# Gating the rows before the experts, one bank for the sum of all experts, and value sums in transpose mode

## The reference, cut to what matters

```python
gate = jnp.einsum('bsd,de->bse', x, W_gate)                 # 8 experts
kth  = jax.lax.top_k(gate, 2)[0][..., -1:]
mask = jax.nn.softmax(jnp.where(gate >= kth, gate, -jnp.inf), axis=-1)
h = jax.nn.relu(jnp.einsum('bsd,edh->bseh', x, W1) + b1)    # 128 -> 512, each expert
y = jnp.einsum('bseh,ehd->bsed', h, W2) + b2                # 512 -> 128
return (y * mask[..., None]).mean(axis=-2)
...
out = jnp.einsum('hbst,hbtd->hbsd', attn, v)                # third block, the value sums
```

## Time and profile before

| | us |
|---|---|
| median of 3 runs | 3009.41 |
| lowest and highest run | 2994.25, 3014.82 |
| the profiled execution, its own time | 3026.84 |
| its span from first to last instruction | 3025.1 |
| PE busy | 2416.5 |
| DVE busy | 1970.3 |
| ACT busy | 1169.0 |
| POOL busy | 649.0 |

### The profile page before, as it was taken

How to read it: one execution, slowest core, us unless ns; L and a number is a source line. 1 busy time by engine, 2 the same in 40 slices (tenths; PEclk the granted TensorE clock), 3 DMA queues, 4 the chain that set the end, 5 groups by cost and what they waited for, 6 DMA issues and landing times.

```text
span 3025.1 us, 42816 instructions
## 1 busy us (share of the span) xinstructions
PE 2416.5 (80%) x11055; PEld 1154.7 (38%) x11055; DVE 1970.3 (65%) x3597; ACT 1169.0 (39%) x2421; POOL 649.0 (21%) x1332
## 2 busy tenths in 40 slices
PE   3888888888888869999888888988888888744444
PEld 1233332333332224444444544554454454323332
DVE  4455555555554422225888778878877877889883
ACT  0444444544444434444344344334434433321122
POOL 3233333333333220000111221211122121110110
PEclk6778777867876769999999999999999999877776
DMA  5432222322222100000000000000010000000000
GB/s 134 105 59 45 44 55 51 69 44 44 53 45 54 23 29 28 28 28 28 29 32 0 31 31 14 17 31 31 0 31 31 14 17 32 4 0 4 3 3 7
DMA packets 87832, 100.79 MB, mean 33 GB/s; under 512 B 11080, under 2 KB 82416, under 8 KB 83568
## 3 DMA queue, kind: packets, MB, share of 16 engines
q1 hardware_dynamic: 80768, 94.41, 12.8%
q10 hardware_dynamic: 6896, 4.38, 0.6%
HBM read 68.35 MB, written 29.62 MB: 32 GB/s over the span
## 4 chain that ended last, share of the span: by engine, by line
DVE 25%; PE 23%; issue 8%; POOL 4%; ACT 3%; DVEq 1%; ACTq 0%; POOLq 0%
PE rest_bank L944 8%; PE rest_bank L951 7%; DVE acc L1197 5%; DVE logits L1158 3%; DVE prod L1156 3%; PE rest_bank L988 3%; ACT y L1344 2%; DVE pos L1173 2%; DVE term L1113 1%; DVE total L1120 1%; POOL rstd2b L1424 1%; POOL rstd2b L1426 1%; DVE stats2b L1069 1%; PE rest_bank L1013 1%; PE rest_bank L965 1%
## 5 line engine op out<-in xcount | busy, mean ns | idle before, releaser
L462 DVE TENSOR_REDUCE maxima<-scores 128x2 f32<-128x1024 f32 (+3 forms) x512 | 415.6, 822 | 407.9 <-PE scores L351 406.9
L944 PE MATMUL rest_bank<-xn_t,w 128*128 128x512 f32 x1024 | 561.4, 635 | 96.6 <-ACT xn_t L1356 75.9
L1411 ACT ACTIVATE hidden<-rest_bank,b 128x512 f32<-128x512 f32 x512 | 349.8, 686 | 619.5 <-PE rest_bank L944 493.2
L951 PE MATMUL rest_bank<-hidden,w 128*128 128x512 f32 x1024 | 532.8, 606 | 3.1 <-DVE term L1113 3.1
L551 ACT ACTIVATE probs<-turned 128x512 f32<-128x512 f32 (+3 forms) x1024 | 396.2, 439 | 347.3 <-PE turned L369 290.3
L369 PE MATMUL turned<-q_stack,k_stack 51*128 51x512 bf16 (+3 forms) x1024 | 267.5, 370 | 140.4 <-DMA q_stack<-max_rows 85.3
L620 POOL TENSOR_SCALAR_AFFINE_SELECT probs<-probs 128x256 f32<-128x256 f32 x512 | 212.0, 415 | 632.2 <-ACT probs L551 632.0
L944 PEld LDWEIGHTS rest_bank<-xn_t,w 128*128 128x128 f32 x1024 | 195.8, 203 | 293.6 <-issue 251.5
L951 PEld LDWEIGHTS rest_bank<-hidden,w 128*128 128x128 f32 x1024 | 199.0, 195 | 253.6 <-issue 248.3
L380 PE MATMUL o_bank<-probs,v_ext 128*32 128x512 f32 (+3 forms) x2048 | 248.9, 567 | 0.5 <-POOL probs L620 0.3
L1423 POOL TENSOR_SCALAR mean_shift<-mv2b 128x4 f32<-128x4 f32 x48 | 11.8, 245 | 1064.1 <-DVE mv2b L1072 1064.1
(11 more groups left out here) (204 smaller groups left out, 3104.6 us busy)
## 6 DMA issues: line engine op xcount, KB each, us to landing
mask_all<-mask_scratch SPq DMA_DIRECT2D x32, 1024.0 KB, 4.7
stack_q<-parts_q SPq DMA_DIRECT2D x96, 128.0 KB, 2.4
stack_k<-parts_k SPq DMA_DIRECT2D x96, 128.0 KB, 2.4
q_stack<-stack_q SPq DMA_DIRECT2D x32, 384.0 KB, 5.7
k_stack<-stack_k SPq DMA_DIRECT2D x32, 384.0 KB, 9.7
x<-in_L_attn_batch_dram SPq DMA_DIRECT2D x16, 256.0 KB, 5.5
w<-in_L_ffn_W_dram ACTq DMA_DIRECT2D x16, 256.0 KB, 3.2
out_dram<-x SPq DMA_DIRECT2D x16, 256.0 KB, 5.0
```

The costliest lines, as they stand in the source:

```text
L462: dve.tensor_reduce(mx[:, w % 2, :, p, qt], s_bank[s % 2][:, :, 0:(qt + 1) * P], AX.X, ALU.max)\
L944: pe.matmul(h_bank[k % 2][:, :], t.w1[:, k // F, (k % F) * P:(k % F + 1) * P], xn1_t[:, :], start=True, stop=True).then_inc(s_h, 1)
L951: pe.matmul(y_bank[k // F % 2][:, :], t.w2[:, k, :], hidden[:, k % 4, :], start=(k % F == 0), stop=(k % F == F - 1))\
L1411: act.activation(hidden[:, k % 4, :], h_bank[k % 2][:, :], ACT.Relu, bias=t.b1[:, k:k + 1])\
```

## The change

Each expert now gets rows that are already multiplied by its gate. DVE makes them (`v_weighted_rows`): (row + 1) times the mask, into one of four buffers `xe`, two parts ahead of use; those for experts 0 and 1 of the next step in part 7, ahead of the last statistics. Because the rows are normalised, their sum over the 128 numbers is zero, so with W1 less its column means plus b1/128 the product with (row + 1) is the old product plus b1. These weights are made once, ahead of step -1 on PE (`pe_biased_weights`, two products of 512 columns for each expert) and in parts 1 to 3 of step -1 on DVE. As the mask isn't negative, relu of the gated rows is the gated relu.

`pe_expert` swaps its operands: `hidden` is loaded as weights, 128 columns at a time, and the piece of W2 streams through, four products a key; all 32 keys of a step add up in one bank, with the gated b2 as four products at key 2. The sum comes out in rows, so the turn of `total` goes; ACT copies the bank to SBUF at the next step's start. ACT's relu has no bias any more. Its copy of the rows moves from the step's start to k = 29 of the step before; the exponential from k = 24 to 20, the mask's turn from key 30 to 24, the gate selection from part 5 to 4 and the mask from part 6 to 5. The value sums get `is_transpose=True`.

```diff
@@ experts_and_mixing @@
-        h_bank, y_bank, m1, ... = banks[0:2], banks[2:4], banks[4], ...
+        h_bank, y_bank, m1, ... = banks[0:2], banks[2], banks[4], ...
+        def pe_biased_weights(pe, e):
+            if e == 0:
+                pe.wait_ge(s_means, 2)
+                pe.wait_ge(s_b1, 16)
+            if e == 7:
+                pe.wait_ge(s_biased, 1)
+            pe.matmul(column_banks[e][:, :], minus_mean, t.w1[:, e, :], start=True, stop=False)
+            pe.matmul(column_banks[e][:, :], plus_mean, b1_row[:, e, :], start=False, stop=True).then_inc(s_columns, 1)
         def pe_hidden(pe, i, k):
-            if k == 0:
-                pe.wait_ge(s_xt, i + 1)
+            if k % F == 0:
+                pe.wait_ge(s_xe, E * i + k // F + 1)
...
-            pe.matmul(h_bank[k % 2][:, :], t.w1[...], xn1_t[:, :], ...
+            pe.matmul(h_bank[k % 2][:, :], t.w1[...], xe[:, k // F % XE, :], ...
+        def pe_expert_biases(pe, i):
+            if not (isinstance(i, int) and i == 0):
+                pe.wait_ge(s_total, i)
+            for j in range(G):
+                pe.matmul(y_bank[:, j * P:(j + 1) * P], mask_t[:, j * P:(j + 1) * P], t.b2[:, :], start=(j == 0), ...
         def pe_expert(pe, i, k):
-            if k % F == 0:
-                pe.wait_ge(s_y_read, 8 * i + k // F + 1)
             pe.wait_ge(s_relu, 32 * i + k + 3)
-            pe.matmul(y_bank[k // F % 2][:, :], t.w2[:, k, :], hidden[:, k % 4, :], start=(k % F == 0), stop=(k % F == F - 1))
+            for j in range(G):
+                mm = pe.matmul(y_bank[:, j * P:(j + 1) * P], hidden[:, k % 4, j * P:(j + 1) * P], t.w2[:, k, :],
+                               start=False, stop=(k == E * F - 1), skip_group_check=True)
-        def pe_experts_out(pe, i):
...
         def pe_mix(pe, i, j):
-                               start=(k == 0), stop=(k == keys - 1))
+                               start=(k == 0), stop=(k == keys - 1), is_transpose=True)
-        def v_expert(dve, own, i, e):
...
+        def v_weighted_rows(dve, i, e):
+            if e == 0:
+                dve.wait_ge(s_mask_lo, 16 * i + 16)
+                dve.wait_ge(s_xt, i + 1)
+            if e == E // 2:
+                dve.wait_ge(s_mask_hi, 16 * i + 16)
+            if not (isinstance(i, int) and E * i + e < XE):
+                dve.wait_ge(s_h, 32 * i + 4 * (e - XE + 1))
+            dve.scalar_tensor_tensor(xe[:, e % XE, :], xn1_t[:, :], 1.0, mask_all[:, e, :], ALU.add, ALU.mult)
+               .then_inc(s_xe, 1)
         def v_experts_stats(dve, own, i):
-            dve.wait_ge(s_m1, before_m1(i) + 1)
-            v_stats1(dve, own, i, 1, lambda j: m1[:, j * P:(j + 1) * P])
+            dve.wait_ge(s_total, i)
+            v_stats1(dve, own, i, 1, lambda j: total[:, j, :])
+        def v_biased_weights(dve, e):
+            dve.wait_ge(s_columns, e + 1)
+            dve.tensor_tensor(t.w1[:, e, :], t.w1[:, e, :], column_banks[e][:, :], ALU.add).then_inc(s_biased, 1)
+        def a_experts_sum(act, i):
+            await_(act, passed["scalar"], s_y, 32 * i + 4)
+            act.activation(total[:, :, :], y_bank[:, :]..., ACT.Copy).then_inc(s_total, 1)
...
         def d_mask(sp, g):
-                await_(sp, passed["sync"], s_y_read, 8 * g - 2)
+                await_(sp, passed["sync"], s_xe, E * g - 4)
...
-                await_(sp, passed["sync"], s_y_read, 8 * g + 2)
+                await_(sp, passed["sync"], s_xe, E * g)
@@ block @@
+                for e in range(E):
+                    pe_biased_weights(pe, e)
                 all_steps(pe, pe_step)
...
+                pool.memset(minus_mean, -1.0 / D).then_inc(s_means, 1)
+                pool.memset(plus_mean, 1.0 / D).then_inc(s_means, 1)
...
+                sp.dma_start(b1_row, a["L0_ffn_b1"].rearrange("(o e) h -> o e h", o=1)).then_inc(s_b1, 16)
```

More of the change, by code:

```diff
@@ L816 @@
 HALVED = (1,)
-STEPS_E, STEPS_P, STEPS_S, STEPS_M, STEPS_Q = 6, 9, 13, 56, 16 + len(HALVED)
+STEPS_P, STEPS_S, STEPS_M, STEPS_Q = 9, 13, 56, 16 + len(HALVED)
+XE = 4
 def masked(value, bits):
@@ L871, in experts_and_mixing @@
         mask_all = sb("mask_all", [P, E, N])
-        hidden, term, total = sb("hidden", [P, 4, N]), sb("term", [P, N]), sb("total", [P, N])
-        y1 = sb("y1", [P, G, D])
+        hidden, xe, total = sb("hidden", [P, 4, N]), sb("xe", [P, XE, N]), sb("total", [P, G, D])
         kv = sb("kv", [P, 2 * S, 2 * D])
@@ L889, in experts_and_mixing @@
         z_t = o_t
+        b1_row = mask_all[0:1, :, :]
+        minus_mean, plus_mean = hidden[:, 3, 0:P], hidden[0:1, 3, P:2 * P]
         def tiles(g):
@@ L1038, in pe_step @@
                     if k == 13:
-                        pe_turn(pe, i, 5, 2)
+                        pe_turn(pe, i, 4, 2)
                     if k == 15:
                         pe_gates(pe, i)
-                    if k == 30:
+                    if k == 24:
                         pe_mask(pe, i)
@@ L1057, in pe_step @@
                 if experts:
+                    if isinstance(i, int) and i == 0 and k == 0:
+                        pe.wait_ge(s_biased, E)
                     if k < E * F:
                         pe_hidden(pe, i, k)
+                    if k == 2:
+                        pe_expert_biases(pe, i)
                     if k >= 2:
@@ L1261, in v_step @@
             for e in range(E):
+                if experts and e + 2 < E:
+                    v_weighted_rows(dve, i, e + 2)
                 if e == 0:
-                    if end:
-                        v_expert(dve, None, i - 1, E - 1)
                     if finish:
@@ L1283, in v_step @@
                         v_kink_heights(dve, i, 1)
+                if isinstance(i, int) and i == -1 and e >= 1:
+                    for n in {1: (0, 1), 2: (2, 3), 3: (4, 5, 6, 7)}.get(e, ()):
+                        v_biased_weights(dve, n)
                 if e == 2:
@@ L1302, in v_step @@
                 if e == 4:
+                    if gates:
+                        v_gates(dve, own_s, i)
                     if finish:
@@ L1311, in v_step @@
                     if gates:
-                        v_gates(dve, own_s, i)
+                        v_mask(dve, own_s, i)
                     if attend:
                         v_positions(dve, own_m, i)
-                if e == 6 and gates:
-                    v_mask(dve, own_s, i)
                 if attend:
@@ L1322, in v_step @@
                         v_softmax(dve, own_m, i)
-                if experts and e >= 1:
-                    v_expert(dve, own_e, i, e - 1)
+                if e == 7 and gates:
+                    v_weighted_rows(dve, i + 1, 0)
+                    v_weighted_rows(dve, i + 1, 1)
                 if e == 7 and finish:
@@ L1328, in v_step @@
                     v_last_add(dve, i, m)
-            assert not experts or own_e.n == STEPS_E, own_e.n
             assert not end or own_p.n == STEPS_P, own_p.n
@@ L1368, in a_step @@
             m = before_m2(i) - (0 if attend else 1) if finish else None
-            if experts:
-                a_expert_rows(act, i)
+            if end:
+                a_experts_sum(act, i)
             for k in range(E * F):
                 if k == 5 and end:
-                    a_scale1(act, i, 1, lambda j: m1[:, j * P:(j + 1) * P], y1).then_inc(s_m1_read, 1)
+                    a_scale1(act, i, 1, lambda j: total[:, j, :], total).then_inc(s_y1, 1)
                 if k == 6 and end:
@@ L1399, in a_step @@
                     a_inner(act, i, k - INNER_AT)
-                if k == 24 and gates:
+                if k == 20 and gates:
                     await_(act, passed["scalar"], s_gated, i + 2)
                     act.activation(gexp[:, :, :], shifted[:, :, :], ACT.Exp).then_inc(s_gexp, 1)
-                if k == 30 and gates:
-                    a_copy(act, mask_t[:, :], m1[0:E, :], s_m1, before_m1(i) + 7, s_m1_read)
+                if k == 24 and gates:
+                    a_copy(act, mask_t[:, :], m1[0:E, :], s_m1, before_m1(i) + 6, s_m1_read)
+                if k == 29 and gates:
+                    a_expert_rows(act, i + 1)
                 if k == 31 and finish:
@@ L1410, in a_step @@
                     await_(act, passed["scalar"], s_h, 32 * i + k + 1)
-                    act.activation(hidden[:, k % 4, :], h_bank[k % 2][:, :], ACT.Relu, bias=t.b1[:, k:k + 1])\
+                    act.activation(hidden[:, k % 4, :], h_bank[k % 2][:, :], ACT.Relu)\
                        .then_inc(s_relu, 1)
@@ L1460, in d_mask @@
             first = isinstance(g, int) and g == 0
-            await_(sp, passed["sync"], s_m1_read, 4 if first else 7 * g)
+            await_(sp, passed["sync"], s_m1_read, 4 if first else 6 * g + 1)
             if not first:
```

90 lines of the change are left out of this document (37 added, 53 removed).

## The result

The changed kernel takes 3021.65 us (median of 19 runs) against 3008.89 for the kernel before on the same chip; the ratio is 1.0058, with a 95% interval of 1.0037 to 1.0080. The changed kernel is slower by 0.6%, within the 1% that the prediction called "same", but 39 us above the predicted 2983.0 and above the range's upper end of 3016.

A forecast was written before the change was run, and what follows sets the result against it. Steady steps were taken as a loop through PE and DVE, with PE bounding steps 0 to 3. Terms -34 - 13.5 - 2.9 + 6.5 + 17.5 = -26.4 us gave a 2983 median; range 2947 to 3016.

The forecast's parts named there:

- The front: From first row statistics to first hidden product: sixteen bias-weight products and the mask's round trip add +17.5 us.
- the mask's way, +7: In the front: the mask's write, spread and one product now stand ahead of the first hidden product, +7 us.
- the 3 to be saved at a higher clock: In the front, from turn to first product: some 3 of 8.7 us saved by a higher PE clock.
- Steady steps: Steps 5 to 14: each wins 3.4 us through lighter DVE work and PE's slack; ten win 34.
- PE's stall at the start: Start of a steady step: PE's 7.28 us wait for ScalarE's copy of the rows goes, but is worth nothing itself.
- Steps 0 to 3: Experts-only steps, PE-bound: step 0 longer by 2.0 us, steps 1 to 3 by 1.5 each, together +6.5.
- The 4.68 stall stays: Step 1, before the turn: PE's 4.68 us wait stays, as the expert sum's scaling starts right behind a late relu.
- The end: Step 15 to the end: value sums as transposes and missing DVE pairs shorten waits, together -13.5 us.
- step 4: Step with experts and logits: DVE pairs go, the mask's small instructions wait for an exponential; -2.9 us, between -5 and 0.
- The second: Front: all sixteen at low clock, +10.5; expert products 0.04 dearer in steps 0 to 4 and behind the turn; chance 0.13.
- The third: Between first value sum and gates: transposes pull the clock down, a step's gain becomes 1.5 us; 3002; chance 0.13.
- The first: Steady steps: less stalling keeps PE's clock up, some 1.8 us a step come back; 2965; chance 0.22.

The follow-up runs named there:

- the grouped run: Changed kernel, b1 products still one-row, but products of one kind together (seven of W1, seven of b1, last two); ratio 0.9992 to the kernel before.
- the split kernel: Changed kernel with b1 spread over 128 rows, seven W1 products ahead of step -1, other nine behind the mask's turn; ratio 0.9943 to the kernel before.

## Why the prediction was wrong

**The front, the step that failed.** The prediction had "at low clock for the first three (1.71 each) and 0.86 for thirteen: 16.3 us", and so the turn 12.4 us later. The sixteen took 32.0 and the turn came 28.7 later (34.4 us after the first row statistics instead of 5.7). That one term is 16 us too small. Its two faults are measured: a busy PE was taken to raise the clock whatever it computes, but with the one-row products between it did not rise, and in the grouped run it fell amid them; and a product's price was taken from rows where 128-row products follow each other, but in alternation it is 0.29 dearer. The upper bound, all sixteen at 1.71, was too low for the second reason. With 128-row products the price was as predicted, 15.9 us. From the turn to the first product it took 15.2 instead of 8.7, +6.5: the mask's way, +7, was right, and the 3 to be saved at a higher clock were not, as the clock stayed at 0.50; even behind the 128-row products, with the full clock for the first 4 us, it took 13.9. The prediction's own terms, 12.4, +7 and -3, add up to 16.4, not to the 17.5 that it wrote.

**Steady steps, -24.1 instead of -34.** Most of the mechanism was right: the first half won, DVE now waits for the result's turn (5.16 where some 3 was said), an expert's eight records take 0.89 us, 16 value-sum records 1.9, the keys-and-values wait fell from 2.10 to 1.27. Wrong was that PE's stall at the start goes and that it "is worth nothing itself". Of 7.28 us 4.43 stayed, as the first relu stands behind the last scale on ScalarE, and the stall leaves its mark on the clock at the step's start: behind it the hidden, b2 and first expert products run at 0.50, so the relu ahead of the scale is late, and the scale and DVE's x add with it. The prediction counted the b2 products at 0.9 (2.07 there) and looked at the scale in step 1 only. With the scale one key earlier the ten steps give 38.0 us against the kernel before, more than predicted.

**Steps 0 to 3, +10.1 instead of +6.5.** "The 4.68 stall stays" was right, it is 4.83, and so was the observation that the scale starts right behind a relu. Not seen was that this is a matter of one key: with the scale a key earlier the four steps take 256.3 us, 0.9 less than before the change. Of the 3.6 us between forecast and measurement 1.6 are step 0, 61.0 us instead of 57.4 where +2.0 was forecast; in the split kernel, where the step begins at the full clock, it takes 59.4, just those +2.0. The other 2.0 were not taken apart further.

**The end, -10.4 instead of -13.5; step 4, -3.6 instead of -2.9.** The transposes give 9.5 of the 10.4. In the last step DVE's wait for a value sum fell from 4.00 to 2.13 and for the projection from 7.42 to 5.73, 3.6 where 5 was said.

**The rivals.** The second, front and expert products dearer, is nearest: for the front its place was right, but its price of 10.5 us for all products at the low clock knew nothing of the alternation, and its dearer expert products did not come. The third's lower clock is there (0.91 over the ten steady steps, 0.94 with products), but not where the third put it, between the first value sum and the gates: it comes behind the gates, in the longer wait for a relu, and costs less than the transposes save. The first, that the clock holds, is what the earlier scale brings about in steps 2 and 3.

## What to carry to other kernels

Before work is put ahead of a chain at the start of a stage, price it at the clock that the stage has there and with its neighbours in order: one-row products among 128-row ones did not keep the clock up here, and each change of rows cost 0.29 us at the low clock; b1 spread over 128 rows by the transfer was cheaper than one row of it. Look for the wait at the end of such a chain, too, and hide the work beside it (here the mask's way through DRAM). And where an engine's order is written out by hand, ask of each wait whether the instruction stands behind one that is late only now: one key on ScalarE was worth some 28 us here.

## What the runs showed of the hardware that was not expected

- 32 us of unbroken products, every other one with a single row, left the granted clock at 0.50, where sixteen of 128 rows had it at 1.00 within the first group. In the grouped kernel it rose to 1.00 during the 128-row products and fell again during the one-row products behind them, without a pause of PE.
- A product whose number of rows differs from that of the one ahead took 2.0 us instead of 1.71 at that clock: its first weights were loaded only about when the product ahead ended.
- Behind the stall of 4.83 us in step 2 the clock had fallen, behind the one of 3.09 not: 1.74 us less of stall were worth 3.9 us of the step.
- With transposes for the value sums the granted clock of the steady steps is lower (0.91 instead of 0.94 in the changed kernel, 0.89 instead of 0.93 in the kernel before), yet in the steps read during the sums it is 1.00: it falls in a wait for a relu that the shorter sums lengthen, from 0.47 to 3.72 us and from 1.48 to 4.01.
